# Two layers on one core: row maxima of two head groups moved into the expert blocks of layer 0

## What is computed

```python
# layer 0 attention, 16 heads of 16
q, k, v = h @ Wq.T, h @ Wk.T, h @ Wv.T;  q, k = rope(q), rope(k)
mem_out = (elu(q)+1) @ ((elu(k)+1).T @ v) / ((elu(q)+1) @ sum(elu(k)+1))
attn = softmax(q @ k.T / sqrt(16)) @ v
attention_out = (g * mem_out + (1 - g) * attn) @ Wo.T
# layer 0 mixture: 8 experts of width 176, two of them per token
y0 = sum over the two chosen experts of w_e * (silu(x @ G_e) * (x @ U_e)) @ D_e
# layer 1: chunked linear attention with decay and gate, then 8 experts of width 512, two per token
```

## Time and profile before

| what | us |
|---|---|
| runs before: median of three | 1045.2 |
| lowest, highest | 1041.05, 1048.74 |
| the profiled execution's own time | 1045.42 |
| its span from first to last instruction | 1043.6 |
| TensorE busy | 878.9 (84%) |
| VectorE busy | 572.6 (55%) |
| ScalarE busy | 406.5 (39%) |
| GpSimd busy | 312.0 (30%) |

### The profile page before, as it was taken

How to read it: one execution, slowest core, us unless ns; L and a number is a source line. 1 busy time by engine, 2 the same in 40 slices (tenths; PEclk the granted TensorE clock), 3 DMA queues, 4 the chain that set the end, 5 groups by cost and what they waited for, 6 DMA issues and landing times. The chain is left out here.

```text
span 1043.6 us, 15136 instructions
## 1 busy us (share of the span) xinstructions
PE 878.9 (84%) x4672; PEld 515.5 (49%) x4672; DVE 572.6 (55%) x1269; ACT 406.5 (39%) x686; POOL 312.0 (30%) x250
## 2 busy tenths in 40 slices
PE   3779999939989998999988857169999999999973
PEld 3755666501224444434434646146666656666652
DVE  7535788347877766678674323624433433343337
ACT  2225566605564566467547504002222222222210
POOL 2022666463001320151015003033333443333231
PEclk9989899955998987998998857569999999999985
DMA  9413455475221423333303303798634445343354
GB/s 276 113 31 122 131 186 184 160 196 139 87 68 52 112 91 122 122 102 111 132 24 110 111 21 122 206 261 259 198 92 92 102 104 119 86 86 92 71 167 146
DMA packets 158770, 130.58 MB, mean 125 GB/s; under 512 B 64288, under 2 KB 140336, under 8 KB 158704
## 3 DMA queue, kind: packets, MB, share of 16 engines
q1 hardware_dynamic: 151552, 110.18, 36.9%
q0 software_dynamic: 7152, 19.54, 6.6%
HBM read 83.67 MB, written 46.01 MB: 124 GB/s over the span
## 5 line engine op out<-in xcount | busy, mean ns | idle before, releaser
L1292 DVE TENSOR_REDUCE b_negmax<-b_psM 128x1 f32<-128x512 f32 x256 | 162.7, 682 | 66.6 <-PE b_psM L1454 64.1
L1223 ACT ACTIVATE b_probs<-b_psE 128x512 f32<-128x512 f32 x256 | 138.8, 595 | 121.6 <-PE b_psE L1472 120.8
L1454 PE MATMUL b_psM<-b_kst,b_qst 96*128 96x512 bf16 x256 | 100.6, 438 | 29.2 <-DMA b_vst<-scratch_v 13.7
L1472 PE MATMUL b_psE<-b_qst,b_kst 98*128 98x512 bf16 x256 | 90.2, 414 | 15.3 <-ACT b_probs L1223 11.0
L1818 POOL DMA_INDIRECT scratch_ys<-d_y,d_put x39 | 40.3, 1034 | 130.5 <-ACT d_y L1855 127.8
L1991 PE MATMUL d_psG<-d_w,d_xT 128*128 x156 | 76.8, 616 | 2.8 <-issue 1.9
L1481 PE MATMUL b_psV<-b_probs,b_vst 128*32 128x512 f32 x512 | 74.9, 658 | 2.9 <-ACT b_probs L1223 2.9
L1824 POOL TENSOR_TENSOR d_rs<-d_ss,d_neghalf 128x16 f32<-128x16 f32 x16 | 47.0, 2938 | 98.9 <-DVE d_ss L1920 98.9
L1999 PE MATMUL d_psU<-d_w,d_xT 128*128 x156 | 74.8, 602 | 0.0
L2016 PE MATMUL d_psY<-d_w,d_hidden 128*128 x312 | 74.8, 382 | 0.0
L1472 PEld LDWEIGHTS b_psE<-b_qst,b_kst 98*128 98x128 bf16 x256 | 20.8, 99 | 107.7 <-ACT b_probs L1223 53.7
(11 more groups left out here) (353 smaller groups left out, 1685.1 us busy)
## 6 DMA issues: line engine op xcount, KB each, us to landing
scratch_parts<-a_parts SPq DMA_DIRECT2D x12, 512.0 KB, 4.3
b_qst<-scratch_parts SPq DMA_DIRECT2D x96, 64.0 KB, 2.3
b_kst<-scratch_parts SPq DMA_DIRECT2D x96, 64.0 KB, 2.3
scratch_parts<-b_part SPq DMA_DIRECT2D x24, 256.0 KB, 3.3
d_qst<-scratch_parts SPq DMA_DIRECT2D x96, 64.0 KB
d_kst<-scratch_parts SPq DMA_DIRECT2D x96, 64.0 KB
scratch_ys<-a_y SPq DMA_DIRECT2D x39, 128.0 KB, 1.7
scratch_v<-a_xn SPq DMA_DIRECT2D x4, 1024.0 KB, 6.8
```

Of the source, the lines that this page charges most:

```text
L1223: nc.scalar.activation(probs[k % PSLOTS][:, h, :], psE[h % 2][:, :], ACT.Exp, scale=float(HD) ** -0.5).then_inc(scores_used[h % 2], 1)
L1292: nc.vector.tensor_reduce(negmax[i][:, t, h:h + 1], psM[:, h % 2, :], AX_X, ALU.max, negate=True).then_inc(rows_used[h % 2], 1)
L1454: nc.tensor.matmul(psM[:, h % 2, :], qst[g][0:STACK, h, t * P:(t + 1) * P], kst[g][0:STACK, h, :], start=True, stop=True).then_inc(rows_re ...
L1472: nc.tensor.matmul(psE[h % 2][:, :], kst[g][0:STACKM, h, k * P:(k + 1) * P], qst[g][0:STACKM, h, :], start=True, stop=True).then_inc(score ...
```

## The change

1. **Logits with the values.** ACT copies all 264 columns into v tiles of that width; DVE reads the logits from there; `project_v` no longer waits for DVE. Same for `rank`.
2. **Inverse earlier.** `invert` stands behind five of the eight halves of `project_qk`, and its wait for the experts' numbers moves to each `mix` (and each `gate` of layer 1).
3. **xgT on ACT.** The copy of L703 moves from DVE to ACT, behind the copy of hT.
4. **Row maxima of groups 0 and 1 of batch 0 in the front.** SP loads their stacks at blocks 16, 18 (group 0) and 24, 26 (group 1) over the finished q and k tiles of batches 0 and 1; 32 products go into the single bank psR: one a block in blocks 21 to 32 (two in 21 and 28), then three a block from block 33. Group 0's maxima are also turned and sent there; group 1's are turned in the middle's loop. POOL sets the two rows of ones.
5. **The middle** starts its loop at once. SP there loads the values of group 0, the identity, group 2, the weights, the constants, the values of group 1, group 3, in this order. DVE's wait for the tables moves behind batch 0. ACT's prelude is unchanged.
6. Stacks, maxima and semaphores are kept over the barrier; memory placement follows.

```diff
 def front_order():
+    rows = [(n, r) for n in range(2) for r in range(TILES * HG)]
+    given = 0
     for b in range(BLOCKS + 1):
+        pace = 0 if b < ROWS_FROM else 1 if b < ROWS_FAST else 3
+        if b % 7 == 0 and ROWS_FROM <= b < ROWS_FAST:
+            pace = 2
         for kind, n in (("mix", b + 1), ("down", b - 1), ("turn_h", b), ("turn", b + 3)):
             if 0 <= n < BLOCKS:
                 order.append((kind, n, 0))
+            if pace and given < len(rows):
+                pace -= 1
+                order.append(("row", *rows[given]))
+                given += 1
+                if given % (TILES * HG) == 0:
+                    order.append(("split", rows[given - 1][0], 0))
+                    if given == TILES * HG:
+                        order.append(("maximum", 0, 0))
...
@@ TensorE, front @@
             def mix(b, _):
+                pe.wait_ge(dispatch.expert_done, 1)
                 owner[b] = pe.value_load(dispatch.expert[0:1, b:b + 1], min_val=0, max_val=E - 1)
...
             if b:
-                    pe.wait_ge(routing.copied, b)
                     pe.wait_ge(v_done, b)
...
+            def row(n, r):
+                t, h = r // HG, r % HG
+                pe.wait_ge(shared.stack_in[n], 16 * 2 * len(Q_PARTS))
+                if n == 0 and r == 0:
+                    pe.wait_ge(dispatch.take_done, 1)
+                elif r:
+                    pe.wait_ge(shared.rows_used[(r - 1) % 2], 8 * n + (r - 1) // 2 + 1)
+                else:
+                    pe.wait_ge(shared.nmT_copied, n)
+                nc.tensor.matmul(psR, qst[n][0:STACK, h, t * P:(t + 1) * P], kst[n][0:STACK, h, :],
+                                 start=True, stop=True).then_inc(shared.rows_ready, 1)
...
-            for i in range(1, 2 * BATCHES):
+            for i in range(1, 5):
                 project_qk(i)
             dispatch.invert(pe)
+            for i in range(5, 2 * BATCHES):
+                project_qk(i)
...
@@ VectorE, front @@
+            def row(n, r):
+                dve.wait_ge(shared.rows_ready, TILES * HG * n + r + 1)
+                nc.vector.tensor_reduce(negmax[n][:, r // HG, r % HG:r % HG + 1], psR, AX_X, ALU.max,
+                                        negate=True).then_inc(shared.rows_used[r % 2], 1)
...
@@ ScalarE, front @@
-                nc.scalar.activation(v[b][:, :, :], psV[:, :, 0:D], ACT.Copy).then_inc(v_done, 1)
+                nc.scalar.activation(v[b][:, :, :], psV[:, :, 0:D + E], ACT.Copy).then_inc(v_done, 1)
...
+            def turn(b, _):
+                act.wait_ge(x_ps, b + 1)
+                if b >= 2:
+                    act.wait_ge(mix_ps, b - 1)
+                nc.scalar.activation(xgT[b % 2].rearrange("p k n -> p (k n)"), psXH[:, 0, 0:KT * P], ACT.Copy).then_inc(xgT_done, 1)
...
@@ SyncE, front @@
+            def maximum(n, _):
+                sp.wait_ge(shared.nmT_copied, n + 1)
+                sp.wait_ge(shared.ones, 2)
+                sp.dma_start(scratch["max"], nmT[n][:, :]).then_inc(shared.max_out, 16)
+                sp.wait_ge(shared.max_out, 16 * (n + 1))
+                sp.dma_start(qst[n][STACK:STACKM, :, :], scratch["max"].rearrange("(a h) t -> a h t", a=2)).then_inc(shared.max_in[n], 16)
...
@@ SyncE, middle @@
-            load(0, 0)
+            load_v(0, 0)
             sp.dma_start(ident[:, :], io["ident"]).then_inc(ident_in, 16)
-            load(0, 1)
+            load(0, 2)
...
-            load(0, 2)
-            send_max(1, 0, 0)
+            load_v(0, 1)
             load(0, 3)
...
@@ TensorE, middle @@
-            for t in range(TILES):
-                rows(0, 0, t, 0, range(HG))
-            pe.wait_ge(identb_done, 1)
-            for t in range(TILES):
-                rows(1, 1, t, 0, range(HG))
-                if t == 0:
-                    turn_max(0, 0)
             pe.wait_ge(ones, GROUPS)
+            pe.wait_ge(ident_in, 16)
```

More of the change, by code:

```diff
@@ L185, in weigh_pair, with __init__, sems @@
                                 ALU.mult).then_inc(self.weighed, 1)
+class Maxima:
+    def __init__(self, nc):
+        def sems(name, n):
+            return [nc.alloc_semaphore(f"{name}{i}") for i in range(n)]
+        self.stack_in, self.max_in, self.rows_used = sems("stack_in", GROUPS), sems("max_in", GROUPS), sems("rows_used", 2)
+        self.max_out, self.rows_ready, self.negmax_hi, self.negmax_parts, self.nmT_ready, self.nmT_copied, self.ones = (
+            nc.alloc_semaphore(n) for n in ("max_out", "rows_ready", "negmax_hi", "negmax_parts", "nmT_ready", "nmT_copied", "ones"))
 class Dispatch:
@@ L502, in _ @@
                 sp.dma_start(dst[:, :], io[src]).then_inc(consts_in, 16)
-            walk({"light": light, "down": down})
+            walk({"light": light, "down": down, "stack": stack, "maximum": maximum})
             for s in range(YSLOTS):
@@ L665, in _ @@
                 copy_qk(i)
-            walk({"light": light, "mix": mix, "turn_h": turn_h, "down": down})
+            walk({"light": light, "turn": turn, "mix": mix, "turn_h": turn_h, "down": down})
         @block.vector
@@ L789, in _, with round_identity @@
             dispatch.tables(dve)
-            walk({"light": light, "turn": turn, "mix": mix})
+            def round_identity():
+                dve.wait_ge(ident_in, 16)
+                nc.vector.tensor_copy(identb[:, :], ident[:, :]).then_inc(identb_done, 1)
+            round_identity()
+            walk({"light": light, "mix": mix, "row": row, "split": split, "maximum": maximum})
         @block.tensor
@@ L917, in _ @@
             project_qk(0)
-            pe.wait_ge(routing.copied, BATCHES)
+            pe.wait_ge(v_done, BATCHES)
             dispatch.rank(pe)
-            for i in range(1, 2 * BATCHES):
+            for i in range(1, 5):
                 project_qk(i)
             dispatch.invert(pe)
-            walk({"light": light, "turn": turn, "mix": mix, "turn_h": turn_h, "down": down})
+            for i in range(5, 2 * BATCHES):
+                project_qk(i)
+            walk({"light": light, "turn": turn, "mix": mix, "turn_h": turn_h, "down": down, "row": row, "maximum": maximum})
 RW = E + HD
```

185 lines of the change are left out of this document (115 added, 70 removed).

## The result

| | before | after |
|---|---|---|
| median of four runs each, us | 1045.88 | 1054.98 |
| lowest to highest | 1041.05 to 1048.74 | 1052.89 to 1057.37 |
| span of the profiled execution | 1043.6 | 1053.7 |

The ratio is 1.0092, with a 95% interval of 1.0048 to 1.0137: slower by 0.9%. All ratios here leave out executions more than 1.5% above the fastest of the same kernel. The forecast was 1048.0 us, with a range of 1032 to 1061. The number lies within 7 us of it, and nearer still to the 1058 that I had given for the clock that falls. The profile shows that it is the sum of a miss of 15 us in one direction and one of 7 in the other.

A forecast was written before the change was run, and what follows sets the result against it. TensorE bounds the front from the first expert blocks to its end; in the middle the maxima finish only 3.3 us after ScalarE's tables. 1045.4 - 11.3 + 1.4 + 5 + 12 - 4.5 = 1048.0 us, range 1032 to 1061.

The forecast's parts named there:

- the clock that falls: Rival: TensorE's clock drops in blocks 34 to 38, +7 us, with two earlier places up to +13; 1058 us; chance 0.20.
- within 1%: Whole kernel: measured time less than about 10 us from no change, given a chance of 0.53.
- Start of the front, change 1: Value projections: no wait for the logits' copy, last copy ends at 36.7 instead of 43.2; gain 6.5 us, bounds 3.5 to 6.5.
- Inverse, change 2: Before the first expert block: first transposes at 61.6 instead of 71.62, gain 10.0 us with change 1 in it.
- The 11.3 of the forecast: Changes 1 and 2 summed: 10.0 us plus 1.3 for half of an avoided low clock; bounds -7 and -12.7.
- xgT on ScalarE: Expert blocks: one more ScalarE copy, about 0.35 us, ahead of exponential steps in four places; +1.4 us, lower bound 0.
- the second rival: Falling clock, here its part at blocks 14 and 22: waits of 1.9 us, about 3 us each; rival's chance 0.20.
- Rows in blocks 21 to 32: Front: 14 row products cost TensorE 3.1 us, a second row's wait +1, VectorE's reductions +1; sum +5, bounds +3.1 and +7.
- Rows from block 33 on: End of front: 18 products through one bank, three a block, stretch a block from 2.83 to 5.5 us; +12, lower bound +6.
- The middle: Stage after the front: constants land at 19.2 us, exponentials start at 28.4 instead of 32.3; -4.5 us, bounds +0.5 and -7.
- The rival of late constants: Middle: constants land 23 us or more after the barrier, prelude late too, no gain there; 1052 us; chance 0.09.
- From the stage after the first batch on everything moves as a block: Rest of the kernel after the first batch's stage: only shifts in time, nothing added to or taken from the sum.

The follow-up runs named there:

- first pair: First profiled traces of the kernel before and the kernel after, unchanged; spans 1043.6 and 1053.7 us.
- second trace of the kernel after: The kernel after run once more, unchanged, timed in turn with the kernel before; ratio 1.0104, span 1066.9 us.
- the head alone: Kernel before with only changes 1 and 2 (logits copied with the values, inverse behind five halves); ratios 0.9882 and 0.9907 in two timings.
- second pair: The kernel before and the kernel after each traced once more, unchanged; spans 1061.9 and 1066.9 us.
- e9_from23: Kernel after with its rows given from block 23 instead of 21, and three a block from block 31 instead of 33; ratio 1.0130.
- e6_const: Kernel after with the middle's constants fetched ahead of its layer 1 weights; ratio 1.0061.

## Why the prediction was right, and where it was not

The total was inside the range and "within 1%" is what was measured. Of the signs that I had named, two of the right outcome came (first transposes near 61.6; blocks of over 5 us with waits for VectorE's maximum and then "issue"), and two of the wrong one: a clock under 1.00 at the end of the front, and constants later than 20 us (20.2 and 22.3). The front's last copy of y was 9 to 15 us later than the 218.6 named. So the total was right, but the rival of the falling clock describes the front better than the forecast does. By the steps:

- **Start of the front, change 1: right.** Last values copy ends at 36.9 (forecast 36.7), and alone it moves the first transposes to 65.09, by the forecast 6.5 us.
- **Inverse, change 2: right.** First transposes at 61.8 (61.6), behind the copy of keys as said. My sum had a slip in it: the inverse, waiting until 51.7 and then taking 1.3, ends at 53.0 and not 52.3. Block 0's y is 9.7 us earlier in the first pair, where the clock fell at the gap of 1.1 us all the same, and 12.7 in the second (81.5 to 68.8), where it did not. From the first transposes to that copy it was 10.6 us with the fall and 7.8 without. Of the ten traces with both changes, six have the fall. The 11.3 of the forecast, which counted half of such a fall, sit between.
- **xgT on ScalarE: right in size.** Blocks 0 to 20 took 67.2 us in the second trace of the kernel after and 66.4 with the head alone (both at the upper level nearly throughout): +0.8, forecast +1.4, and no more than two traces of one kernel differ by. In the first pair it was 73.7 against 69.7, where the clock fell behind two of the waits, as the second rival had it.
- **Rows in blocks 21 to 32: the term that failed, "TensorE is full: 14 x 0.22, sum +5, bounds 3.1 and 7".** From block 20 to 32: +10.2 in the first pair, +14.8 in the second. I had costed a row by the work that it adds to each engine. Its real price is the tie: TensorE waits for a maximum that queues behind whatever VectorE is held by. In the second pair 7 of the 14.8 us are one such wait with its clock fall (block 20 to 21, 10.0 us for 2.8, and 2.8 again in e9_from23). Both measured values lie outside the bounds.
- **Rows from block 33 on: right mechanism, too small: "12", measured 17.4 and 16.9** (block 32 to 38, 35.7 us against 18.3 and 18.8). A block at the upper level took 5.24 us (y copies of blocks 33 and 34 at 205.50 and 210.74, and at 200.08 and 205.32 in the second trace; forecast 5.5), with "issue" waits of 0.4 to 0.5 in place of the 1.1 that I read from the earlier trace rows. The rest is the lower level of the clock, 0.50 to 0.61 in three stretches. That is the rival "the clock falls", with its place right and its price (+7) about as found, by my estimate: 17 less 12, plus what I had over for "issue".
- **The middle: right in size, the path only in part.** Gain from the last copy of y to the first group's result 4.6 in the first pair and 5.4 in the second (4.5). All seven traces with the old middle take 52.2 to 58.1 us for it, and the six with the new one, e6_const left out, 49.2 to 51.7. But the constants landed at +20.2 and +22.3 (19.2), and the exponentials began at +29.3 and +31.4 (28.4), where the two traces before have +32.3 and +32.1. So in the second pair the earlier exponentials gave 0.7 of the 5.4 us and not 3.9. The first load came 0.9 us sooner behind the last copy of y, and from the exponentials to the first result it was 16.6 us in place of 20.5, for a reason that stays open. The rival of late constants had come half true there: taking the constants from behind the weights gives 7 us.
- **"From the stage after the first batch on everything moves as a block": failed.** From the first group's result to the end the kernel after is 7.3 us shorter in the first pair and 9.3 in the second. That the change does this is unlikely: over all runs this stretch takes 772.0 to 797.0 us in the seven traces with the old middle and 770.5 to 791.4 in the seven with the new one. In the six traces whose groups run shortest, the 16 groups take 324.7 to 329.2 us (from the first to the last), with no order by kernel: 327.2 before, 324.7 after, 327.6 with the head alone, 329.2 with the rows from block 23. The stretch from the last group to layer 1's first probabilities takes from 76.9 us (after) to 81.7 (before) in them, and 81.3 with the logits alone. In the two second traces it is 78.1 before and 77.1 after. Whether the kernel before is regularly the longer one there stays open.

So the right total owes something to luck: the front was 14.8 us dearer than said (21.9 against 7.1), and 7.3 came back where I had counted nothing. Of the gain that was sought, the head gives its 10 us and the middle 5; 32 products, which had cost the middle 3 us of ScalarE's wait, cost the front 24 to 32 us (block 20 to the last copy of y: 87.0 to 91.5 us in the traces of the kernel after's front, 59.7 to 63.1 in the three with the head and no rows). This price includes the loads of the stacks and the turn of the maxima, which no run takes apart.

## What to carry to other kernels

Work moved under another stage's cover is to be priced by the dependence that it adds, not by its busy time: a product whose bank must come back from VectorE before the next puts TensorE one VectorE queue behind, and a delay that was hidden before (here VectorE's product held up beside GpSimd) becomes TensorE's idle time, in several places here with a stretch at the lower clock behind it. Ask of the stretch that loses the work what would end last there without it; here the maxima ended only 3 us after ScalarE's tables, so their 22 us of VectorE work promised little more than those 3. When a change has several parts, time the part without a new dependence by itself: here it is 1% faster, and the whole 0.9% slower.

## What the runs showed that was not expected

- VectorE's two-input operations on SBUF took up to 3.8 us in place of 1.2 where GpSimd's 2.1 us subtraction and gathers fell on them; this happens in the kernel before too (3.17 us at 123.44), hidden.
- The same program's span was 1043.6 us in one trace and 1061.9 in another, and its runs in three sets had medians from 1044.5 to 1061.0. The 16 groups of the middle differ by more than the whole (327 against 349 us), at a mean granted clock of 0.92 against 0.88, with longer waits at a few places.
- A wait of 2.19 us at the same instruction was followed by a fall of the clock in one trace of the kernel after (0.52 from 93.5 to 103.5) and not in the other (1.00).
